# Writing a local-attention mask with four quarter-array matmuls in place of two full-array ones

## What is computed

```python
bk, bv = (look_around(bk), look_around(bv))   # window before, then this one: 128 keys
sim = jnp.einsum('bhwid,bhwjd->bhwij', bq, bk)
mask = (i < j) | (i > j + WINDOW) | (j == -1)
sim = jnp.where(mask, -jnp.finfo(sim.dtype).max, sim)
attn = jax.nn.softmax(sim, axis=-1)
out = jnp.einsum('bhwij,bhwjd->bhwid', attn, bv)
```

## Time and profile before

| | |
|---|---|
| median of three runs | 3085.78 us |
| span of the profiled execution | 3084.0 us |
| PE (TensorE) busy in it | 2726.9 us |
| DVE (VectorE) | 2071.2 us |
| ACT (ScalarE) | 1795.1 us |
| POOL (GpSimd) | 867.2 us |
| mean granted TensorE clock | 0.939 |

### The profile page before, as it was taken

The page is one execution under the profiler, slowest core; times in us unless marked ns, Lnnn a source line. Parts: engine busy times, 40 slices in busy tenths (PEclk is TensorE's granted clock), DMA queues, the critical chain, the costliest instruction groups (busy, mean ns, idle before and its releaser), DMA issues. The chain is left out here.

```text
span 3084.0 us, 67656 instructions
## 1 busy us (share of the span) xinstructions
PE 2726.9 (88%) x25880; PEld 2025.6 (66%) x25880; DVE 2071.2 (67%) x6099; ACT 1795.1 (58%) x3611; POOL 867.2 (28%) x876
## 2 busy tenths in 40 slices
PE   6867999999589999999999999999998567999965
PEld 5755577777356666666666666666666356999943
DVE  4545544444356876677766786668765478999998
ACT  1132355555256666666666666666665368888876
POOL 2222400000212222232232322222221244333377
PEclk8767999999799999999999999999999768999987
DMA  6110144444100000000000000000000003666611
GB/s 194 28 21 21 32 134 133 138 137 143 42 10 16 12 5 16 16 16 12 5 16 16 15 10 8 16 16 12 1 12 12 6 29 99 200 202 195 192 41 45
DMA packets 104318, 175.10 MB, mean 57 GB/s; under 512 B 16416, under 2 KB 73280, under 8 KB 103872
## 3 DMA queue, kind: packets, MB, share of 16 engines
q1 hardware_dynamic: 95808, 153.98, 16.8%
q0 software_dynamic: 8192, 16.79, 1.9%
HBM read 131.00 MB, written 26.74 MB: 51 GB/s over the span
## 5 line engine op out<-in xcount | busy, mean ns | idle before, releaser
L1938 POOL TENSOR_TENSOR l_rinv<-l_ssm,w_neg_half 128x8 f32<-128x8 f32 x128 | 210.0, 1641 | 613.6 <-DVE l_ssm L2223 613.5
L247 PE MATMUL bank<-l_kT,l_qT 32*128 32x128 f32 (+1 forms) x3072 | 359.6, 352 | 1.7 <-DVE l_qm L1309 1.6
L247 PE MATMUL bank<-l_qm,l_kT 32*128 32x128 f32 (+1 forms) x3072 | 355.9, 349 | 0.8 <-DVE l_qm L2134 0.4
L1968 ACT ACTIVATE l_probsT<-bank 128x768 f32<-128x768 f32 x256 | 207.8, 812 | 203.2 <-PE bank L247 202.4
L266 DVE TENSOR_REDUCE l_tops<-bank 128x2 f32<-128x256 f32 (+1 forms) x384 | 196.5, 512 | 183.2 <-PE bank L247 180.1
L235 PE MATMUL bank<-masks,ident 128*128 128x256 bf16 x1536 | 242.1, 275 | 32.6 <-DVE l_tops L267 30.5
L247 PEld LDWEIGHTS bank<-l_kT,l_qT 32*128 32x128 f32 x3072 | 203.6, 187 | 84.6 <-issue 66.0
L2601 DVE RECIPROCAL l_rden<-l_den 128x256 f32<-128x256 f32 x128 | 224.0, 1750 | 30.8 <-ACT l_den L2528 30.3
L825 POOL DMA_INDIRECT back<-sorted_y,pos x128 | 125.5, 980 | 423.2 <-DMA sorted_y<-l_y_tile 390.1
L267 DVE TENSOR_REDUCE l_tops<-bank 128x2 f32<-128x512 f32 (+1 forms) x384 | 227.6, 593 | 0.0
L235 PEld LDWEIGHTS bank<-masks,ident 128*128 128x128 bf16 x1536 | 143.6, 98 | 120.4 <-DVE l_tops L267 86.9
(11 more groups left out here) (337 smaller groups left out, 7321.5 us busy)
## 6 DMA issues: line engine op xcount, KB each, us to landing
l_expert<-in_experts SPq DMA_DIRECT2D x72, 768.0 KB, 4.1
l_expert<-in_experts SPq DMA_DIRECT2D x72, 578.0 KB, 3.5
l_x_tile<-sorted_x SPq DMA_DIRECT2D x144, 64.0 KB, 4.1
sorted_y<-l_y_tile SPq DMA_DIRECT2D x144, 64.0 KB, 3.8
l_v_half<-l_v SPq DMA_DIRECT2D x32, 264.0 KB, 3.2
sorted_x<-x_all SPq DMA_DIRECT2D x18, 256.0 KB
l_v_half<-l_v SPq DMA_DIRECT2D x32, 132.0 KB, 3.1
l_x<-in_x SPq DMA_DIRECT2D x8, 256.0 KB, 4.1
```

The lines of the kernel that those rows point to most:

```text
L247: lasts.append(pe.matmul(bank[:, at:at + n * P], lhs[:, c * P:(c + 1) * P], rhs[:, x0 * P:(x0 + n) * P], start=False, stop=(i == 1), skip_ ...
L1938: pool.tensor_tensor(rinv[:, i, :], ssm[:, i, :], g.neg_half[:, 0:LH], ALU.pow).then_inc(rinv_ready[l], 1)
L1968: Bt.took(act.activation(probsT[:, (j // 2) % 2, 2 * (j % 2):2 * (j % 2) + 2, :], two[:, :, 0:AW], ACT.Exp), rd, use)
```

## The change

The mask tile of the local attention becomes two tiles, one for each `side`. In each, the 64 rows of that side's mask stand twice, in partitions 0 to 63 and in 64 to 127. In place of one matmul for each head with the whole identity (128 by 128) there are two for each head with a 64 by 64 block of it: rows `64*i`, columns `64*side`, bank `i`, 256 columns. The values written are the same. The constant that holds the masks grows from three to four tiles of 384 columns, in HBM, in SBUF as f32 and in bf16. The order: both heads of side 0, then both of side 1. The matmuls of the scores and all other code stay.

```diff
-                    for i in range(2):
-                        pe.matmul(two[:, i, 0:S], g.ident16[:, :], g.mask_local[:, :], start=True, stop=False,
-                                  skip_group_check=True)
+                    for side in range(2):
+                        for i in range(2):
+                            part = slice(LD * i, LD * (i + 1))
+                            pe.matmul(two[LD * side:LD * (side + 1), i, 0:S], g.ident16[part, part], g.mask_local[part, side, :],
+                                      start=True, stop=False, skip_group_check=True)
...
-        "alibi": (1, [P, NG, S]), "masks": (0, [P, 3, AW]),
+        "alibi": (1, [P, NG, S]), "masks": (0, [P, 4, AW]),
...
-        masks16 = ctx.enter_context(nc.sbuf_tensor("masks16", [P, 3, AW], BF16))
+        masks16 = ctx.enter_context(nc.sbuf_tensor("masks16", [P, 4, AW], BF16))
...
-        g.mask_causal, g.mask_anti, g.mask_local = masks16[:, 0, :], masks16[:, 1, :], masks16[:, 2, 0:S]
+        g.mask_causal, g.mask_anti = masks16[:, 0, :], masks16[:, 1, :]
+        g.mask_local = masks16[:, 2:4, 0:S]
...
-            masks32 = c0.enter_context(nc.sbuf_tensor("masks32", [P, 3, AW], FP32))
+            masks32 = c0.enter_context(nc.sbuf_tensor("masks32", [P, 4, AW], FP32))
...
-    c["masks"] = np.stack([np.concatenate(x, 1) for x in
-                           ((causal, zero, causal), (anti, zero, anti), (first, window, zero))], 1).astype(np.float32)
+    local = np.concatenate((first, window, zero), 1)
+    sides = [np.tile(local[y * WINDOW:(y + 1) * WINDOW], (P // WINDOW, 1)) for y in range(2)]
+    c["masks"] = np.stack([np.concatenate(x, 1) for x in ((causal, zero, causal), (anti, zero, anti))] + sides,
+                          1).astype(np.float32)
```

## The result

The changed kernel took 3068.71 us in the median of five runs (3060.01 to 3073.03), the kernel before 3085.78 beside it (3074.12 to 3086.51): a ratio of 0.9955 with a 95% interval from 0.9937 to 0.9974. The forecast was 3073 us, in a range from 3062 to 3085. The profiled span went from 3084.0 to 3066.0 us, by 18.0, where 12.8 was forecast.

A forecast was written before the change was run, and what follows sets the result against it. TensorE, busy 88% of the span, was taken to set the pace. Fourteen rounds at 0.87 us give 12.2, plus 0.5 and 0.3, less 0.2 for the constant: 12.8 us off 3085.8, so 3073 us, range 3062 to 3085.

The forecast's parts named there:

- the rival by which all of the gain arrives: Third layer's local masks: every pair's saving reaches the end, 20.8 us in all, 3065 us; chance 0.10.
- The prediction's own sign for that rival: A round of the third layer shortening by 1.3 us would show that the steps forecast as absorbed count too.
- The switch of 0.09: TensorE at the local masks: each change of array shape leaves 0.09 us empty; the change moves it ahead of the masks.
- four quarters cost one stream: At L1693 the four quarter-array masks of a pair overlap, costing 0.11 us, with 0.05 for weights in the open.
- The rival of row halves that take turns: At the masks, row halves don't overlap for bf16: four take 0.22 us, gain 3 us, 3082 us; chance 0.12.
- quarters one after the other: At the masks, quarters don't overlap at all: four take 0.43 us, about 15 us lost, 3101 us; chance 0.06.
- The price of a pair: TensorE saving per pair's masks: 0.11 us after full-array work, 0.21 after another shape, about 0.22 after a wait.
- Step 16 gives nothing: A round's first local pair gains 0.21 us on TensorE but loses it at L247, waiting for VectorE's earlier-started work.
- Step 17 gives nothing: A round's second local pair gains 0.21 us, then loses it at L1684 behind ScalarE's unbroken chain to L2013.
- Steps 18 to 23 arrive whole: A round's last six local pairs keep their gains: 0.21, 0.11, 0.22 and 3 x 0.11, 0.87 us a round.
- step 23: A round's last local pair, the tightest place: slack 0.14 us behind L1989, gain 0.11, so it still passes.
- the mild case of the rival: Third layer's clock falls in 5 more rounds, costing 8 us, 3081 us; the rival of more falls has chance 0.10.

The follow-up runs named there:

- run 7: Kernel before, with the rotation's two products ahead of the masks of step 16 cut to one column instead of 32: 97.77 us a round, ratio 0.9955.
- run 8: Changed kernel, with the rotation's two products ahead of the masks of step 16 cut to one column instead of 32: 96.25 us a round, ratio 0.9886.
- run 1: Kernel before, with each pair's local masks written by four half-array matmuls (128 rows, 64 columns): 98.48 us a round, ratio 1.0061.
- run 5: Changed kernel with the four quarter masks in the other order, both sides of head 0 first: 96.75 us a round, ratio to before 0.9942.
- run 6: Changed kernel with every quarter-array mask written twice, eight matmuls a pair: 97.40 us a round, ratio to before 1.0034.
- the kernels with the exchange: Both kernels with a projection moved to step 14 and transposes to 15: before 99.64 us a round, ratio 1.0088; changed 98.10, ratio 1.0061.
- run 4: Kernel before with full-array masks everywhere, but five tiles of mask constant instead of three: 97.93 us a round, ratio 0.9993.
- run 2: Changed kernel, but full-array masks in steps 16 and 17 and a fifth constant tile: 96.85 us a round, ratio to before 0.994.
- the repeat: Changed kernel and kernel before measured again, unaltered, on one chip: 96.72 against 97.92 us a round, ratio 0.9955.

## Why the prediction was right, point by point

**What bounds it**: right. PE's instructions became shorter, and the end moved with them.

**The total alone proves little.** 3068.7 us lies between the forecast of 3073 and the 3065 of the rival by which all of the gain arrives, and nearer to the latter; with 12 us between runs no total could choose. The rounds do: every pair counting would have given about 1.55 us a round by the prices measured here, as it did in runs 7 and 8; 1.15 was measured. The prediction's own sign for that rival, 1.3 us a round, was not reached, but 1.15 is nearer to it than to the forecast 0.87.

**The switch of 0.09 is moved, not removed, and four quarters cost one stream**: right, by runs 1, 5 and 6. The rival of row halves that take turns and that of quarters one after the other have fallen: four masks span 0.30 us in both orders.

**The price of a pair** was a little off: 0.11 forecast after full-array work, 0.14 to 0.15 measured (1.40 less 1.26); 0.21 after another shape, 0.25 measured. The term mis-sized is the load of the masks' weights in the open. I took 0.05 from the f32 scores; the first score comes 0.13 after the masks, so it is at most 0.13 - 0.11 = about 0.03. The bounds were 0.01 and 0.05. Over steps 18 to 23 this makes some 0.2 us a round.

**Step 16 gives nothing**: right, shown by the wait of 0.28 for VectorE, which run 8 removes.

**Step 17 gives nothing**: wrong by 0.10. The step that failed is the sentence that ScalarE is in one unbroken chain from L1989 to the end of L2013. ScalarE of the changed kernel in order of time:

```profile
1359.52 1.16 ACT L1991 ACTIVATE l_probs<-bank,l_negmax 128x128 f32<-128x128 f32 x4
1360.53 0.73 ACT L2015 ACTIVATE l_kT<-bank,w_one_rows 128x512 f32<-128x512 f32 x1
```

Counted from the masks of step 16, L1991 is where it was, and L2015 (then L2013) starts 9.69 after them instead of 9.83. It starts 0.15 *before* its predecessor ends (1359.52 + 1.16 = 1360.68), as ScalarE instructions behind this line do elsewhere in these traces (0.14 for the L2035 of rows 11 and for the L2039 behind the L1989 of rows 12, in the kernel before). In the kernel before it started just when its predecessor ended. The predecessor on ScalarE there, and the keys on PE that L2013 copies, before and after:

```profile
1367.72 1.16 ACT L1989 ACTIVATE l_probs<-bank,l_negmax 128x128 f32<-128x128 f32 x4
```

```profile
1368.24 0.61 PE L1835 MATMUL bank<-w_ident,l_cums 128*128 128x128 f32 x4
```

```profile
1359.88 0.61 PE L1837 MATMUL bank<-w_ident,l_cums 128*128 128x128 f32 x4
```

L2013 started at 1368.88, 0.03 behind the end of L1835 (1368.85), and L2015 at 1360.53, 0.04 behind that of L1837 (1360.49). So what looked like a full queue was a wait for PE's L1835, up to 0.15 long, hidden because the view calls an engine idle only when none of its instructions runs. What of step 17's gain got past VectorE (0.14, as L1818 shows) moved L2013; L2015 itself then took 0.73 instead of 0.69, and 0.10 arrived. Over the fourteen rounds 1.4 us. The longer wait that the prediction expected at the L1684 of step 17 didn't come.

**Steps 18 to 23 arrive whole**: right to within 0.04 us a round. Even step 23, with a slack of 0.14 by my reading, passed 0.14 to 0.15.

**The sum**: 0.87 forecast a round, 1.15 measured; the difference is 0.10 for step 17 and about 0.2 for the weights. In all fourteen rounds that is 16.1 against 12.2. Two falls more of the clock took 3.0 back in the profiled run, and the earlier start of the third layer, which is chance, gave 2.8: that these two cancel is luck. The half rounds and the closing one, an estimate of 0.8, gave 0.8 and 0.7, and 0.4 more came in what follows.

**The clock**: open, and here the prediction's own sign of being wrong, more falls in the third layer, did come. Where the clock fell it went to 0.50, the 1.2 GHz level, for 3.4 us (busy time by stretch, the changed kernel):

```profile
1649.30:1652.70 3.40, 3.40 (x13) 2.64 (x11) 0.00 (x0) 2.32 (x7) 0.00 (x0) 0.50 0.00 0
```

Such a round took 98.2 to 98.4 us instead of 96.77, so a fall costs 1.4 to 1.6. In the fourteen rounds it fell once in one profile of the kernel before and not at all in the other, three times and twice in those of the changed kernel; the kernels with the exchange, with their longer wait, had 8 and 12. The Trainium skill (TensorE: Matmul & The Clock Gate, Part 1) has the clock halved by default and released by activity, which agrees in direction. That the change itself brings the two more may be, but isn't shown: run 4, with full-array masks, had 11 falls in its fourteen rounds, and run 2, with quarter masks in six steps of eight, had 4 beside it. The mean granted clocks of all executions don't decide it either: 0.936 for the changed kernel (nine) against 0.940 (twenty) in the repeat, but 0.935 for run 5 (four) against 0.933 (fifteen), and they hold much else: in the four traces 178 to 215 us of half clock lie ahead of the third layer and 172 to 184 behind the fourteen rounds, against 0 to 10 in them. By its size, 3.0 us, it is less than the mild case of the rival (8 us).

## What to carry to other kernels

Before a small TensorE matmul that prepares a bank for others, ask whether it can have their shape: a switch of shape cost 0.09 us each time here, and quarters on different rows and columns share one stream's time (0.30 us for four, 0.41 where the shape was 128 by 64). Then walk one period of the loop on every engine and ask at each gain which wait behind it was started by work from *before* it; a step whose neighbours wait for such work gives nothing, whatever its own saving. And when reading whether an engine is "continuously busy", compare each start with the start that its predecessor allows, not with the predecessor's end.

## What the runs showed of the hardware that was not expected

- Quarter-array bf16 weights (64 by 64) cost at most about 0.03 us in the open here (an estimate from 0.13 less a stream of 0.11), against 0.05 for f32 weights of the same shape and 0.01 for full-array bf16 ones. The Trainium skill (TensorE: Matmul & The Clock Gate, "LDWEIGHTS (loading the stationary operand)") gives columns divided by 1.2 in ns, an estimate of 0.053 us for 64 columns; the time in the open measured here is half of that, and decides. That page's fast load asks for 128 columns and a type other than f32 ("Weight-path perf modes"), where the prediction says 2-byte data; for bf16 it is the same.
- Four quarter-array bf16 matmuls that write two banks at the full rate run side by side (0.30 us for four, 0.296 for one), in either order.
- In the first eight experiments, rounds with GpSimd's gathers took 2.3 us and more longer than in the other runs, while rounds without them agreed to 0.03 us (the kernel before: a median of 3135 to 3137 us there, 3080 to 3086 elsewhere). In run 4 PE waited 19.9 us, 11 times between 1000 and 2300 us, for ScalarE's copy of the transposed queries and keys, a wait that the kernel before doesn't have. Why was not tried.
